# Windowed and latent attention in a macaron network: scores by query in two pairs of head groups, latent jobs first, maxima in three bf16 parts

## The chip, the cores and the metric

One core of a Trainium2 chip runs the whole program. The metric is device time in microseconds, from the start to the end of one execution. The changed kernel is timed against the kernel before on the same chip.

## The reference, cut to what matters

The network is x + 0.5 ffn, x + attention, x + 0.5 ffn, then a ternary layer, a relative-position attention and the ternary layer again. The change lies in the first attention (4 batches of 1024 rows, 256 features). For 16 heads of 16 features it computes, with windows of 64 rows:

```python
Q, K, V = x @ wq, x @ wk, x @ wv                     # 16 heads
sc = Q . K / 4 over this window of 64 keys and the one before, band mask j > i and j <= i + 64
local = softmax(sc) @ V                              # the first window has no window before it
GQ = x @ wgq; GK, GV = pool16(x @ wgk), pool16(x @ wgv)   # 8 latent heads, 64 latents
rem = softmax(GQ . GK / 4, latents of later chunks masked) @ GV @ r_out_w
out = (sigmoid(Q . gl) * local + sigmoid(Q . gr) * rem) @ w_out
```

## The kernel before, in words

The layer is `local_phase` (L387). Four engines run programs written out by hand that meet through semaphores; nothing is reordered. Per batch there are four stages.

**Scores by query.** Eight jobs n = (g, m, e): g is the half of the rows (4 tiles of 128), (m, e) picks four of the 16 heads, one in each row group c of 32 partitions. `scores` (L813) fills the four PSUM banks R[:, 0..3]: a mask matmul for each bank with all 128 rows of the array (L823), then 32 fp32 matmuls of 32 rows and 64 columns (L829), which run as 64 passes. VectorE's `top` (L637) takes the maximum over the keys of all four banks at once (L642). `scores` of the next job waits for it, since it writes the same banks. After each job TensorE runs one of the projections that are left (`project`, L776; the first `EARLY` = 8 of 16 ran in the last stage of the batch before), then `turn_tops` turns the maxima. Two latent jobs follow (`latent_scores` L843, `latent_top` L644).

**Scores by key.** `by_key` (L869), for the same eight jobs: mask (L879), minus the maxima spread over the keys by a selecting matmul in fp32 (`sel`, `mT`, L882), and the scores again with keys on the partitions (L888). ScalarE takes the exponential of the four banks in one instruction (L587). `values` (L905) multiplies with V, VectorE copies (`take`, L652), TensorE turns back (`back`, L930), VectorE divides and gates (`normed`, L664). PSUM Z has four banks for everything that is not scores. The two latent jobs are jobs 8 and 9; their `take` is a reciprocal of 512 elements a row and a product.

**Out.** For 8 tiles `remote`, `turn_out`, `project_out` on TensorE, with the next batch's first 8 projections between them.

The masks are made once, by GpSimd, before batch 0.

Of the kernel before, what the change touches and what calls it, by code (L numbers as in the profile page):

```python
# [7 lines left out]
ALU = mybir.AluOpType  # L8
# [378 lines left out]
def local_phase(nc, G, A):  # L387

    with ExitStack() as ctx:
# [22 lines left out]
        sel = sb("sel", [P, 4, P])  # L412
        sel2 = sb("sel2", [P, 2, NL])
        identb = sb("identb", [P, P], BF)
        maskS = sb("maskS", [P, 2, 512], BF)
        maskT = sb("maskT", [P, 2, 512], BF)
        lmaskS = sb("lmaskS", [P, TPB, P], BF)
        lmaskT = sb("lmaskT", [P, S], BF)
# [13 lines left out]
        mt = sb("mt", [P, TPB, P])  # L432
        mtl = sb("mtl", [P, TPB, P])
        mT = sb("mT", [P, S])
        mTl = sb("mTl", [P, S])
# [13 lines left out]
                 "S smax mtr mTe LS lmax ltr lTe ST sexp PV ot rcp back ri norm E o2 o F Fe out res sums stat")  # L449
# [9 lines left out]
        LAST_V, GATE_JOB, Q_LAST = 11, 12, 6  # L459
# [28 lines left out]
        NMASK = 15  # L488

        @block.gpsimd  # L490
        def _(pool):
            nc.gpsimd.memset(blk[:, :], 1.0).then_inc(s["zero"], 1)
            pool.wait_ge(s["zero"], 1)
            c = Count(s["masks"])

            def keep(t, op, fill, base, pattern, multiplier):
                step(pool, nc.gpsimd.affine_select(out=t, in_=t, compare_op=op, fill=fill, base=base, pattern=pattern,
                                                   channel_multiplier=multiplier), c)
# [8 lines left out]
            nc.gpsimd.memset(mt[:, :, :], 0.0)  # L507
            nc.gpsimd.memset(mtl[:, :, :], 0.0)
            nc.gpsimd.memset(onesB[:, :], 0.0)
            for t in (maskS, maskT, lmaskS):  # L510
                nc.gpsimd.memset(t[:, :, :], 0.0)
            nc.gpsimd.memset(lmaskT[:, :], 0.0).then_inc(s["zero"], 1)
            pool.wait_ge(s["zero"], 3)
            for half in range(2):
                rows = slice(WIN * half, WIN * half + WIN)
                keep(maskS[rows, :, :], ALU.is_gt, NEG, 0, [[0, 8], [1, P]], -1)
                keep(maskS[rows, :, :], ALU.is_ge, NEG, WIN, [[0, 8], [-1, P]], 1)
                keep(lmaskT[rows, :], ALU.is_ge, NEG, 0, [[1, S]], -CHUNK)
            keep(maskT[:, :, :], ALU.is_gt, NEG, 0, [[0, 16], [-1, WIN]], 1)
            keep(maskT[:, :, :], ALU.is_ge, NEG, WIN, [[0, 16], [1, WIN]], -1)  # L520
            keep(lmaskS[:, :, :], ALU.is_ge, NEG, 0, [[P, TPB], [0, 2], [-CHUNK, NL]], 1)
            step(pool, nc.gpsimd.memset(onesB[0:WIN, 0:HD], 1.0), c)
            step(pool, nc.gpsimd.memset(onesB[WIN:P, HD:32], 1.0), c)
            step(pool, nc.gpsimd.memset(maskS[0:WIN, 1, 0:WIN], NEG), c)
            step(pool, nc.gpsimd.memset(maskT[0:WIN, 1, 0:WIN], NEG), c)

        @block.scalar
        def _(act):
# [30 lines left out]
            def top_row(b, g):  # L559
                act.wait_ge(s["mtr"], 2 * b + g + 1)  # L560
                copy(mT[:, 512 * g:512 * g + 512], Z[:, 3, :]).then_inc(s["mTe"], 1)

            def latent_top_row(b, g):
                act.wait_ge(s["ltr"], 2 * b + g + 1)
                copy(mTl[:, 512 * g:512 * g + 512], Z[:, 2, :]).then_inc(s["lTe"], 1)
# [3 lines left out]
            act.wait_ge(s["sels"], 5)  # L569
# [3 lines left out]
            for b in range(B):  # L573
                for j in range(EARLY, NPJ):
                    evacuate(b, j)
                    if j == 13:
                        act.wait_ge(s["pj_d"], dves(b, GATE_JOB))
                        nc.scalar.activation(gt[:, :, :, :], gt[:, :, :, :], ACT.Exp, scale=-1.0).then_inc(s["gexp"], 1)
                for g in range(2):
                    top_row(b, g)  # L580
                for g in range(2):
                    latent_top_row(b, g)
                for n in range(NST):
# [3 lines left out]
                    nc.scalar.activation(PT[:, n % 2, :, :], R[:, :, :], ACT.Exp, scale=0.25).then_inc(s["sexp"], 1)  # L587
                    if b + 1 < B and 4 <= n < 8:
                        xT_out(b + 1, n - 4)
# [7 lines left out]
        def _(dve):  # L597
# [39 lines left out]
            def top(b, n):  # L637
                g, m, e = job(n)
                dve.wait_ge(s["S"], b * NJ + n + 1)
                dst = mt[:, :, :].rearrange("p t (c q) -> p c t q", c=4)[:, :, 4 * g:4 * g + 4, 2 * m + e]  # L640
                src = R[:, :, :].rearrange("p c (t k) -> p c t k", t=4)
                nc.vector.tensor_reduce(dst, src, AX.X, ALU.max, negate=True).then_inc(s["smax"], 1)  # L642

            def latent_top(b, g):  # L644
                dve.wait_ge(s["LS"], 2 * b + g + 1)
                for e in range(2):
                    dst = mtl[:, :, :].rearrange("p t (c q) -> p c t q", c=4)[:, :, 4 * g:4 * g + 4, e]
                    src = R[:, :, :].rearrange("p c (t e n) -> p c t e n", t=4, e=2)[:, :, :, e, :]
                    ins = nc.vector.tensor_reduce(dst, src, AX.X, ALU.max, negate=True)
                ins.then_inc(s["lmax"], 1)  # L650

            def take(b, n):  # L652
                dve.wait_ge(s["PV"], b * NST + n + 1)
                if n < NJ:
                    if n >= 2:
                        dve.wait_ge(s["back"], b * NJ + n - 1)
                    copy(OT[:, n % 2, :], Z[:, 2, :]).then_inc(s["ot"], 1)
                else:
                    nc.vector.reciprocal(rcp[:, n % 2, :], Z[:, 3, :]).then_inc(s["norm"], 1)
                    dve.wait_ge(s["norm"], b * NST + n + 1)  # L660
                    at = (n - NJ) * 512
                    nc.vector.tensor_tensor(remT[:, at:at + 512], Z[:, 2, :], rcp[:, n % 2, :], ALU.mult).then_inc(s["ot"], 1)
# [51 lines left out]
            do(nc.vector.tensor_copy(sel[:, :, :], selr[:, 0:4].unsqueeze(2).to_broadcast([P, 4, P])), "sels", 3)  # L714
            do(nc.vector.tensor_copy(sel2[:, :, :], selr[:, 0:2].unsqueeze(2).to_broadcast([P, 2, NL])), "sels", 4)
            do(nc.vector.tensor_copy(identb[:, :], G.ident[:, :]), "sels", 5)
# [8 lines left out]
            pool_rows(0)  # L725
            dve.wait_ge(s["zero"], 3)
            for b in range(B):
                for n in range(NJ):
                    top(b, n)
                    if n == 5:  # L730
                        evacuate(b, GATE_JOB)
                for g in range(2):
                    latent_top(b, g)
# [3 lines left out]
                for n in range(NST):  # L737
                    if 1 <= n <= NJ:
                        normed(b, n - 1)
                    take(b, n)  # L740
                    if b + 1 < B and n < 4:
                        normalise(b + 1, 2 * n)
                        normalise(b + 1, 2 * n + 1)
                    if b + 1 < B and n == 8:
                        pool_rows(b + 1)
                dve.wait_ge(s["norm"], (b + 1) * NST)
# [14 lines left out]
        def _(pe):  # L761
            mm = nc.tensor.matmul

            def turn(b, g4):
# [4 lines left out]
                elif b >= 1:  # L769
                    pe.wait_ge(s["pj_a"], acts(b - 1, NPJ - 1))  # L770
                    pe.wait_ge(s["pj_d"], dves(b - 1, NPJ - 1))
                for q in range(4):
# [1712 lines left out]
```

## Time and profile before

| | us |
|---|---|
| median of 3 runs | 2364.99 (2362.94 to 2365.01) |
| the profiled execution | 2365.43 |
| its span | 2363.7 |
| scores by query of batch 0, 1, 2, 3 start at | 215.0, 364.2, 507.3, 650.5 |
| the same layer's last output tile is added at about | 791 |

The layer's four batches take 576 us of the span: 149.2, 143.1, 143.1 and 140.8. In rows of a timeline the first number is the start in us from the span's start, the second the duration of the merged instructions from the first start to the last end, then engine, line, operation, tiles, shape and count; brackets give the idle time of the engine before and what ended it. 32*64 means 32 rows and 64 columns of the array. The profile models the ends of matmuls: four of 0.38 us each start 0.22 us apart, so starts are compared, not ends.

### The profile page before, as it was taken

Reading aid. Unit: us, or ns where it says so; the run is one execution under the profiler, and the core shown is the slowest. Engines: PE = TensorE matmul, PEld = TensorE weight load, DVE = VectorE, ACT = ScalarE, POOL = GpSimd, SP = SyncE. Lnnn points to the kernel's source line nnn. Section 1 sums busy time; section 2 is a strip of 40 time slices with the busy share of each in tenths; the row PEclk is TensorE's granted clock in tenths of the full one; section 3 lists DMA queues with packets and bytes.
Section 4 is the critical chain, followed back from the end, with each engine's and each line's share of the span. In section 5 each row is a group of like instructions: output and inputs, shape, how many; then the busy total and the mean of one; then the engine's idle time right before and its main releaser. Section 6 shows DMA issues by size and latency. Waiting matters only on the chain. (4 is left out here: it accounts for less than half of the span.)

```text
span 2363.7 us, 74441 instructions
## 1 busy us (share of the span) xinstructions
PE 2036.5 (86%) x32280; PEld 1279.6 (54%) x32280; DVE 1633.0 (69%) x2585; ACT 1220.4 (52%) x1830; POOL 492.8 (21%) x794
## 2 busy tenths in 40 slices
PE   4986888898888797589986999999999999999985
PEld 2653555555555465445873555555555555555544
DVE  6775355364542677866756888888888888888847
ACT  3761231312212476422423777767776777767754
POOL 0002000000000000000013354435443454445420
PEclk7997899999999899699995999999999999999997
DMA  3001000000000000044358445555554455545412
GB/s 109 1 1 34 13 2 20 2 19 3 1 19 2 1 1 6 1 120 148 142 210 253 112 129 132 133 135 142 136 142 123 118 139 142 136 119 137 109 38 72
DMA packets 273791, 195.11 MB, mean 83 GB/s; under 512 B 206744, under 2 KB 260310, under 8 KB 273210
## 3 DMA queue, kind: packets, MB, share of 16 engines
q1 hardware_dynamic: 262586, 139.27, 23.2%
q0 software_dynamic: 10496, 50.75, 5.7%
q8 instruction: 256, 4.19, 0.8%
q14 instruction: 69, 0.57, 0.1%
q10 hardware_dynamic: 384, 0.33, 0.0%
HBM read 91.69 MB, written 93.88 MB: 79 GB/s over the span
## 5 line engine op out<-in xcount | busy, mean ns | idle before, releaser
L2098 DVE TENSOR_REDUCE a1c_nm<-a1c_S 128x1 f32<-128x1024 f32 x512 | 609.6, 1218 | 83.7 <-PE a1c_S L2185 83.2
L2032 ACT ACTIVATE a1c_PT<-a1c_ST 128x1024 f32<-128x1024 f32 x499 | 509.8, 1022 | 65.9 <-PE a1c_ST L2185 63.0
L2049 ACT ACTIVATE a1c_Pb<-a1c_S,a1c_nm 128x192 f32<-128x192 f32 (+1 forms) x512 | 212.3, 415 | 202.2 <-DVE a1c_nm L2098 201.0
L1971 POOL TENSOR_TENSOR a1c_lt<-a1c_lt 128x256 f32<-128x256 f32 (+5 forms) x448 | 254.0, 567 | 35.5
L2088 DVE COPY a1c_PbT<-a1c_T 96x512 f32<-96x512 f32 x256 | 175.8, 687 | 99.4 <-PE a1c_T L2217 97.0
L2185 PE MATMUL a1c_ST<-a1c_Q,a1c_KR 57*128 57x256 f16 (+2 forms) x1066 | 176.3, 285 | 28.9 <-ACT a1c_PT L2032 19.6
L2185 PE MATMUL a1c_S<-a1c_KR,a1c_Q 54*32 54x512 f16 (+13 forms) x2816 | 181.9, 317 | 14.0 <-DMA a1c_Gx<-a_bias 11.4
L2185 PE MATMUL a1c_S<-a1c_KL,a1c_Q 54*32 54x512 f16 (+11 forms) x3136 | 193.4, 326 | 0.3
L2185 PE MATMUL a1c_S<-a1c_Gx,ident 64*32 64x96 f32 (+2 forms) x4352 | 186.0, 242 | 0.0
L1963 POOL DMA_DIRECT2D a_band<-a1c_Pb x128 | 71.1, 555 | 495.5 <-ACT a1c_Pb L2049 495.4
L2217 PE MATMUL a1c_T<-ident,a1c_Pb 128*96 128x128 f32 x1024 | 169.3, 289 | 0.8 <-DVE a1c_mhl L2112 0.8
L2185 PE MATMUL a1c_ST<-a1c_Q,a1c_KL 57*128 57x128 f16 (+1 forms) x932 | 149.9, 266 | 17.8 <-ACT a1c_PT L2032 16.8
L1055 POOL PARTITION_ALL_REDUCE b_wall<-b_wsum x2 | 0.8, 404 | 785.9 <-DVE b_wsum L1100 785.9
L2217 PEld LDWEIGHTS a1c_T<-ident,a1c_Pb 128*96 128x96 f32 x1024 | 102.7, 129 | 88.8 <-issue 55.7
L587 ACT ACTIVATE a_PT<-a_R 128x2048 f32<-128x2048 f32 x40 | 75.1, 1878 | 146.1 <-PE a_R L888 124.0
L312 DVE TENSOR_TENSOR f_hlo<-f_h,f_hhi 128x512 f16<-128x512 f32 x128 | 88.0, 687 | 70.2 <-ACT f_hhi L230 70.2
L2185 PEld LDWEIGHTS a1c_S<-a1c_Gx,ident 64*32 64x32 f32 x4352 | 126.3, 110 | 13.9 <-issue 0.7
L225 ACT ACTIVATE f_h<-f_psH,b,a 128x512 f32<-128x512 f32 x128 | 99.3, 776 | 60.8 <-PE f_psH L336 59.3
L2185 PE MATMUL a1c_PV<-a1c_PT,a1c_VL 128*17 128x512 f32 (+3 forms) x1280 | 127.4, 470 | 0.2 <-issue 0.2
L2185 PE MATMUL a1c_PV<-a1c_PT,a1c_VU 128*17 128x512 f32 (+3 forms) x1280 | 127.5, 470 | 0.0
L642 DVE TENSOR_REDUCE a_mt<-a_R 128x16 f32<-128x2048 f32 x32 | 73.4, 2293 | 73.9 <-PE a_R L829 73.9
L347 PE MATMUL f_psY<-sw2T,f_hhi 128*128 128x256 f16 x512 | 118.7, 273 | 1.0 <-DVE f_hlo L312 1.0
(353 smaller groups left out, 4088.0 us busy)
## 6 DMA issues: line engine op xcount, KB each, us to landing
a_band<-a1c_Pb POOLq DMA_DIRECT2D x128, 384.0 KB, 3.5
a_bias<-a1b_G SPq DMA_DIRECT2D x32, 768.0 KB, 9.3
a1c_Gx<-a_bias SPq DMA_DIRECT2D x128, 192.0 KB, 4.3
a1c_Dt<-a_band SPq DMA_DIRECT2D x128, 126.0 KB, 3.4
a1c_Q<-a_qk SPq DMA_DIRECT2D x192, 64.0 KB
a1c_Vw<-a_values SPq DMA_DIRECT2D x64, 102.0 KB, 3.0
a1c_KL<-a_qk SPq DMA_DIRECT2D x96, 64.0 KB
a1c_KR<-a_qk SPq DMA_DIRECT2D x90, 64.0 KB
```

What stands on the lines that cost most here:

```text
L225: nc.scalar.activation(h[:, n % NB, :], psH[:, n % NB, :], ACT.Gelu, bias=G.b1[:, m:m + 1], scale=G.a1[:, m:m + 1]).then_inc(s["h"], 1)
L312: nc.vector.tensor_tensor(hlo[:, n % NB, :], h[:, n % NB, :], hhi[:, n % NB, :], ALU.subtract).then_inc(s["hlo"], 1)
L347: last = nc.tensor.matmul(psY[:, i % 2, t, :], x[:, n % NB, t * P:t * P + P], G.sw2T[:, m, :], start=(m + part + t % 2 == 0), stop=(m == M ...
L587: nc.scalar.activation(PT[:, n % 2, :, :], R[:, :, :], ACT.Exp, scale=0.25).then_inc(s["sexp"], 1)
L642: nc.vector.tensor_reduce(dst, src, AX.X, ALU.max, negate=True).then_inc(s["smax"], 1)
L1971: add = lambda o, x, y: nc.gpsimd.tensor_tensor(o, x, y, ALU.add)
L2032: nc.scalar.activation(PT[:, q % 8, :, :], place(q), ACT.Exp).then_inc(s["exp"], 1)
L2049: nc.scalar.activation(Pb[:, band_slot(I, c), w0:w1], SP[:, t % 2, I * P - 32 + w0:I * P - 32 + w1], ACT.Exp, bias=nm[:, t // 16 % 2, col: ...
L2088: nc.vector.tensor_copy(PbT[:, e % RING, :], T[0:BW, :]).then_inc(s["Tb_ev"], 1)
L2098: nc.vector.tensor_reduce(nm[:, t // 16 % 2, col:col + 1], SP[:, t % 2, :], AX.X, ALU.max, negate=True).then_inc(s["max"], 1)
L2185: return nc.tensor.matmul(out, w, x, start=start, stop=stop, skip_group_check=True)
L2217: ins = nc.tensor.transpose(T[0:BW, at:at + P], Pb[:, band_slot(I, c), BW * ch:BW * ch + BW], G.ident[:, :])
```

## The change

- **Order.** The two latent jobs come first: `latent_scores` before the eight jobs by query, latent jobs 0 and 1 of `by_key`, `values` and `take`, local jobs 2 to 9. The job list is put in another order, so that the pooled, latent and first V projections are among the early eight, and two each of Q and K later.
- **Pairs.** In `scores` the four row groups are done as two pairs a = 0, 1. Each pair waits for the maxima of its own pair of the job before, writes its masks and its 16 matmuls, and signals by itself; `top` and `latent_top` reduce in two halves; the exponential is two instructions of half the size, and `by_key` masks each pair of banks behind its own half.
- **Masks.** The band is written by matmuls with 64 rows (`ones64`, `band`) on rows 0 to 63 for even c and 64 to 127 for odd c; in jobs with g = 0 each is followed by a further matmul of 64 rows and 64 columns (`wall`) that masks the missing first window. Latent masks take 32 rows (`of16`, `later`, `laterT`).
- **Maxima.** VectorE splits each maximum in three bf16 parts with four small operations (`in_three`); `mt`, `mT`, `sel`, `sel2` and the turning matmuls are bf16.
- GpSimd makes the new masks in 24 steps in place of 15.

```diff
-        JOBS = [("q", 0, 0), ("k", 0, 0), ("q", 1, 0), ("k", 1, 0), ("q", 0, 1), ("k", 0, 1), ("q", 1, 1), ("k", 1, 1),
-                ("v", 0, 0), ("v", 2, 0), ("v", 4, 0), ("v", 6, 0), ("gate", 0, 0), ("g", 0, 0), ("gq", 0, 0), ("gq", 0, 1)]
+        JOBS = [("q", 0, 0), ("k", 0, 0), ("q", 1, 0), ("k", 1, 0), ("g", 0, 0), ("gq", 0, 0), ("gq", 0, 1), ("v", 0, 0),
+                ("q", 0, 1), ("k", 0, 1), ("q", 1, 1), ("k", 1, 1), ("gate", 0, 0), ("v", 2, 0), ("v", 4, 0), ("v", 6, 0)]
...
             def top(b, n):
                 g, m, e = job(n)
-                dve.wait_ge(s["S"], b * NJ + n + 1)
-                dst = mt[:, :, :].rearrange("p t (c q) -> p c t q", c=4)[:, :, 4 * g:4 * g + 4, 2 * m + e]
+                dst = mx[:, :, :, :].rearrange("p t c q -> p c t q")[:, :, 4 * g:4 * g + 4, 2 * m + e]
                 src = R[:, :, :].rearrange("p c (t k) -> p c t k", t=4)
-                nc.vector.tensor_reduce(dst, src, AX.X, ALU.max, negate=True).then_inc(s["smax"], 1)
+                for a in range(2):
+                    dve.wait_ge(s["S"], 2 * (b * NJ + n) + a + 1)
+                    nc.vector.tensor_reduce(dst[:, 2 * a:2 * a + 2], src[:, 2 * a:2 * a + 2], AX.X, ALU.max, negate=True
+                                            ).then_inc(s["smax"], 1)
...
+            def in_three(whole, left, parts, n, name, value):
+                do(copy(parts[:, :, :, 0:n], whole), name, value + 1)
+                do(nc.vector.tensor_tensor(left, whole, parts[:, :, :, 0:n], ALU.subtract), name, value + 2)
+                do(copy(parts[:, :, :, 4:4 + n], left), name, value + 3)
+                nc.vector.tensor_tensor(parts[:, :, :, 8:8 + n], left, parts[:, :, :, 4:4 + n], ALU.subtract).then_inc(s[name], 1)
...
+            def tri(c):
+                return slice(WIN * (c % 2), WIN * (c % 2) + WIN)
+
             def scores(b, n):
                 g, m, e = job(n)
-                if n == 0:
-                    pe.wait_ge(s["res"], b * TPB)
-                    pe.wait_ge(s["pj_a"], acts(b, EARLY - 1))
-                    pe.wait_ge(s["pj_d"], dves(b, EARLY - 1))
-                else:
-                    pe.wait_ge(s["smax"], b * NJ + n)
+                if n % 2 == 0:
+                    pe.wait_ge(s["pj_a"], acts(b, EARLY + n - 3 if n >= 4 else 3))
+                    pe.wait_ge(s["pj_d"], dves(b, EARLY + n - 3 if n >= 4 else 3))
                 K = KO if e else KE
-                for c in range(4):
-                    mm(R[:, c, :], identb[:, :], maskS[:, int(g == 0), :], start=True, stop=False, skip_group_check=True)
-                for t in range(4):
-                    for half in range(2):
-                        at = (4 * g + t) * P + WIN * half
-                        for c in range(4):
-                            rows = slice(32 * c, 32 * c + 32)
-                            ins = mm(R[WIN * half:WIN * half + WIN, c, t * P:t * P + P], QT[rows, m, at:at + WIN],
-                                     K[rows, m, at:at + P], start=False, stop=True, skip_group_check=True)
-                ins.then_inc(s["S"], 1)
+                for a in range(2):
+                    if n == 0:
+                        pe.wait_ge(s["lmax"], 4 * b + 3 + a)
+                    else:
+                        pe.wait_ge(s["smax"], 2 * (b * NJ + n) - 1 + a)
+                    for c in (2 * a, 2 * a + 1):
+                        mm(R[:, c, :], ones64[tri(c), 0:2, :].rearrange("p a x -> p (a x)"),
+                           band[tri(c), :, :].rearrange("p a x -> p (a x)"), start=True, stop=False, skip_group_check=True)
+                        if g == 0:
+                            mm(R[0:WIN, c, 0:WIN], ones64[tri(c), 0, :], wall[tri(c), :], start=False, stop=False,
+                               skip_group_check=True)
+                    for t in range(4):
+                        for half in range(2):
+                            at = (4 * g + t) * P + WIN * half
+                            for c in (2 * a, 2 * a + 1):
+                                rows = slice(32 * c, 32 * c + 32)
+                                ins = mm(R[WIN * half:WIN * half + WIN, c, t * P:t * P + P], QT[rows, m, at:at + WIN],
+                                         K[rows, m, at:at + P], start=False, stop=True, skip_group_check=True)
+                    ins.then_inc(s["S"], 1)
...
-                    ins = nc.tensor.transpose(Z[:, 3, q * P:q * P + P], mt[:, 4 * g + q, :], G.ident[:, :])
+                    ins = mm(Z[:, 3 - g, q * P:q * P + P], mt[:, 4 * g + q, :, :].rearrange("p c x -> p (c x)"), identb[:, :],
+                             start=True, stop=True, skip_group_check=True)
...
-                    mm(R[:, c, :], identb[:, :], lmaskS[:, 4 * g:4 * g + 4, :].rearrange("p t n -> p (t n)"), start=True,
+                    rows = slice(32 * c, 32 * c + 32)
+                    if g == 1 and c % 2 == 0:
+                        pe.wait_ge(s["lmax"], 4 * b + 1 + c // 2)
+                    mm(R[:, c, :], of16[rows, 0:P], later[rows, 4 * g:4 * g + 4, :, :].rearrange("p t e n -> p (t e n)"), start=True,
                        stop=False, skip_group_check=True)
...
+            def by_key(b, n):
+                for c in range(4):
+                    rows = slice(32 * c, 32 * c + 32)
+                    if c % 2 == 0:
+                        if n == 0:
+                            pe.wait_ge(s["smax"], 2 * (b * NJ + NJ) - 1 + c // 2)
+                        else:
+                            pe.wait_ge(s["sexp"], 2 * (b * NST + n) - 1 + c // 2)
+                    if n < 2:
+                        mm(R[:, c, :], laterT[rows, n, :], of16[rows, :], start=True, stop=False, skip_group_check=True)
+                        continue
+                    mm(R[:, c, :], band[tri(c), 0, :], ones64[tri(c), :, :].rearrange("p a x -> p (a x)"), start=True, stop=False,
+                       skip_group_check=True)
+                    if job(n - 2)[0] == 0:
+                        mm(R[0:WIN, c, 0:WIN], wall[tri(c), :], ones64[tri(c), 0, :], start=False, stop=False, skip_group_check=True)
...
+                for g in range(2):
+                    latent_scores(b, g)
+                    project(b, EARLY + g)
                 for n in range(NJ):
                     scores(b, n)
-                    project(b, EARLY + n)
+                    if n < 6:
+                        project(b, EARLY + 2 + n)
+                    if n == 1:
+                        turn_latent_tops(b)
                     if n == 5:
                         turn_tops(b, 0)
-                latent_scores(b, 0)
-                turn_tops(b, 1)
-                latent_scores(b, 1)
-                turn_latent_tops(b, 0)
-                turn_latent_tops(b, 1)
                 for n in range(NST + 2):
                     if n < NST:
                         by_key(b, n)
-                    if 2 <= n < NJ + 2:
-                        back(b, n - 2)
+                    if n == 0:
+                        turn_tops(b, 1)
+                    if n >= 4:
+                        back(b, n - 4)
...
```

## Rows read from the trace of the kernel before

**Rows 1.** Page, part 2: GpSimd and granted TensorE clock, span in 40 slices of 59 us.

```profile
...
POOL 0002000000000000000013354435443454445420
PEclk7997899999999899699995999999999999999997
...
```

**Rows 2.** Stretches (start:end, length, busy PE, PEld, DVE, ACT, POOL, clock, DMA): batch 1, two of batch 3.

```profile
...
364.20:411.80 47.60, 39.81 (x712) 26.09 (x713) 24.81 (x19) 6.51 (x14) 0.00 (x0) 1.00 0.11 24
411.80:458.60 46.80, 43.03 (x1099) 31.47 (x1096) 14.40 (x52) 17.41 (x12) 0.00 (x0) 1.00 0.01 3
458.60:468.50 9.90, 8.20 (x118) 3.89 (x117) 3.12 (x14) 4.32 (x3) 0.00 (x0) 1.00 0.01 2
468.50:478.10 9.60, 5.36 (x32) 1.13 (x32) 6.75 (x6) 0.03 (x1) 0.00 (x0) 0.82 0.01 2
478.10:507.30 29.20, 27.22 (x100) 16.08 (x96) 18.88 (x43) 7.68 (x16) 0.00 (x0) 1.00 0.00 1
699.70:722.40 22.70, 20.18 (x362) 13.30 (x359) 3.39 (x9) 6.23 (x4) 0.00 (x0) 0.70 0.01 2
770.80:792.00 21.20, 16.02 (x67) 12.55 (x64) 16.74 (x42) 3.07 (x8) 0.00 (x0) 0.82 0.00 1
...
```

**Rows 3.** Timeline, batch 1: last mask, second job by query, next mask; gate projection.

```profile
...
369.44 0.38 PE L823 MATMUL a_R<-a_maskS,a_identb 128*128 128x512 bf16 x1
...
369.75 1.21 PE L829 MATMUL a_R<-a_KO,a_QT 32*64 32x128 f32 x64
...
370.89 1.99 PE L795 MATMUL a_Z<-a_wv,a_xT 128*128 128x256 f32 x8
...
371.00 2.29 DVE L642 TENSOR_REDUCE a_mt<-a_R 128x16 f32<-128x2048 f32 x1 [2.27 <-PE a_R L829]
...
373.35 1.04 PE L823 MATMUL a_R<-a_maskS,a_identb 128*128 128x512 bf16 x4 [0.47 <-DVE a_mt L642]
...
384.58 3.76 PE L809 MATMUL a_Z<-a_gates,a_QT 128*128 128x32 f32 x32
...
```

**Rows 4.** Timeline, batch 1: a job by key, with what follows it.

```profile
...
417.70 1.04 PE L879 MATMUL a_R<-a_maskT,a_identb 128*128 128x512 bf16 x4 [2.00 <-ACT a_PT L587]
...
418.67 1.14 PE L882 MATMUL a_R<-a_mT,a_sel 32*128 32x512 f32 x8
...
419.63 1.91 PE L888 MATMUL a_R<-a_QT,a_KO 32*128 32x64 f32 x64
...
421.61 1.88 ACT L587 ACTIVATE a_PT<-a_R 128x2048 f32<-128x2048 f32 x1 [3.96 <-PE a_R L888]
...
422.70 0.69 DVE L598 COPY a_OT<-a_Z 128x512 f32<-128x512 f32 x1 [9.38 <-PE a_Z L918]
...
427.31 0.66 PE L937 MATMUL a_Z<-ident,a_OT 128*128 128x128 f32 x4
...
```

**Rows 5.** Timeline, batch 1: latent scores and their maxima; the end of the batch.

```profile
...
403.11 1.17 PE L855 MATMUL a_R<-a_GKB,a_GQT 32*128 32x128 f32 x32
...
404.35 2.36 DVE L649 TENSOR_REDUCE a_mtl<-a_R 128x16 f32<-128x1024 f32 x2 [2.56 <-PE a_R L855]
...
468.48 1.07 PE L923 MATMUL a_Z<-a_PT,a_onesB 128*32 128x512 f32 x8 [1.31 <-DVE a_loc L676]
...
470.46 3.36 DVE L659 RECIPROCAL a_rcp<-a_Z 128x512 f32<-128x512 f32 x1 [2.13 <-PE a_Z L926]
...
474.65 1.94 PE L923 MATMUL a_Z<-a_PT,a_onesB 128*32 128x512 f32 x8 [4.24 <-DVE a_remT L662]
...
```

**Rows 6.** Timeline, relative attention: a matmul of 64x128 tiles, then of 64x32.

```profile
...
1702.12 0.27 PE L2185 MATMUL a1c_ST<-a1c_Q,a1c_KL 56*128 56x256 f16 x1
1702.33 0.31 PE L2185 MATMUL a1c_S<-a1c_KR,a1c_Q 54*32 54x320 f16 x2
...
```

**Rows 7.** Page, part 5: an exponential of 1024 elements a row.

```profile
...
L2032 ACT ACTIVATE a1c_PT<-a1c_ST 128x1024 f32<-128x1024 f32 x499 | 509.8, 1022 | 65.9 <-PE a1c_ST L2185 63.0
...
```

**Rows 8.** DMA issues of the layer: count, KB, median us to landing.

```profile
...
a_Vp<-a_V SPq DMA_DIRECT2D x4, 544.0 KB, 6.7
...
```

More of the change, by code:

```diff
@@ L411, in local_phase @@
         selr = sb("selr", [P, 32])
-        sel = sb("sel", [P, 4, P])
-        sel2 = sb("sel2", [P, 2, NL])
+        sel4 = sb("sel4", [P, 4])
+        sel = sb("sel", [P, 4, P], BF)
+        sel2 = sb("sel2", [P, 2, NL], BF)
         identb = sb("identb", [P, P], BF)
[L415 to L418, printed above, removed]
+        ones64 = sb("ones64", [P, 8, WIN], BF)
+        band = sb("band", [P, 4, P], BF)
+        wall = sb("wall", [P, WIN], BF)
+        of16 = sb("of16", [P, 512], BF)
+        later = sb("later", [P, TPB, 2, NL], BF)
+        laterT = sb("laterT", [P, 2, P], BF)
         xn = sb("xn", [P, TPB, D])
@@ L644, in latent_top @@
             def latent_top(b, g):
                 dve.wait_ge(s["LS"], 2 * b + g + 1)
[L646 to L650, printed above, removed]
+                dst = mxl[:, :, 4 * g:4 * g + 4, :].rearrange("p c t e -> p c (t e)")
@@ L652, in take, with split_top, split_latent @@
+            def split_top(b, g):
+                dve.wait_ge(s["smax"], 2 * (b * NJ + 4 * g + 4))
+                rows = slice(4 * g, 4 * g + 4)
+                in_three(mx[:, rows, :, :], rest[:, rows, :, :], mt[:, rows, :, :], 4, "split", 8 * b + 4 * g)
+            def split_latent(b):
+                dve.wait_ge(s["lmax"], 4 * b + 4)
+                in_three(mxl[:, :, :, :].rearrange("p c t e -> p t c e"), rest[:, :, :, 0:2], mtl[:, :, :, :], 2, "lsplit", 4 * b)
             def take(b, n):
@@ new lines, in by_key @@
+            def by_key(b, n):
+                for c in range(4):
+                    rows = slice(32 * c, 32 * c + 32)
+                    if c % 2 == 0:
[10 more added lines that the diff above has]
+                        mm(R[0:WIN, c, 0:WIN], wall[tri(c), :], ones64[tri(c), 0, :], start=False, stop=False, skip_group_check=True)
+                if n < 2:
+                    at = n * 512
+                    pe.wait_ge(s["lTe"], 2 * b + 2)
+                    for c in range(4):
+                        rows = slice(32 * c, 32 * c + 32)
+                        mm(R[:, c, :], sel2[rows, :, :].rearrange("p e n -> p (e n)"), mTl[rows, at:at + 512], start=False,
+                           stop=False, skip_group_check=True)
+                    for c in range(4):
+                        rows = slice(32 * c, 32 * c + 32)
+                        ins = mm(R[:, c, :], GKB[rows, :], GQT[rows, at:at + 512], start=False, stop=True,
+                                 skip_group_check=True)
+                else:
+                    g, m, e = job(n - 2)
@@ L876, in by_key @@
                     pe.wait_ge(s["mTe"], 2 * b + g + 1)
                     K = KO if e else KE
-                    for c in range(4):
-                        mm(R[:, c, :], identb[:, :], maskT[:, int(g == 0), :], start=True, stop=False, skip_group_check=True)
                     for c in range(4):
@@ L981, in _ @@
                         by_key(b, n)
[L982 to L983 removed]
+                    if n == 0:
+                        turn_tops(b, 1)
+                    if n >= 4:
+                        back(b, n - 4)
                     if 1 <= n <= NST:
                         values(b, n - 1)
[L986 to L987 removed]
+                    if b + 1 < B and 5 <= n < 9:
+                        turn(b + 1, n - 5)
                 for t in range(TPB + 2):
```

220 lines of the change are left out of this document (110 added, 110 removed).

## The prediction

> **What bounds it now.** I first read the page's slices of the granted clock [rows 1]: the layer lies between 215 and 791 us, and its slices stand at 0.6 to 0.9 in places and at 9 or more elsewhere. Then I cut batch 1 into its stages [rows 2]. By query, 47.6 us, TensorE busy for 39.8 and VectorE for 24.8; by key, 46.8, TensorE busy 43.0; the two latent jobs 9.9; a tail of 9.6 in which TensorE is busy for 5.4 only; the out stage 29.2, TensorE busy 27.2. So TensorE leads nearly everywhere, but two chains stand in its way, which the timeline shows. By query [rows 3]: masks start at 373.35, having waited for the maximum that began at 371.00 and takes 2.29. By key [rows 4]: the masks at 417.70 waited 2.00 for the exponential of 1.88. In the tail [rows 5] TensorE stands idle for 4.24 behind a reciprocal of 3.36, and the next matmuls take 1.94 instead of 1.07, since the clock has fallen to its lower level, 1.2 GHz (0.82 in the mean of that stretch [rows 2]).
>
> **Prices from rows.** A full mask starts 0.22 after the one before ((1.04 - 0.38) / 3 [rows 3]). A change of the array's tiling costs a pause: the last mask starts at 369.44 and the first 32*64 load at 369.75, 0.31 later where 0.22 is the mask's own [rows 3]: 0.09, and the fp32 weights, now uncovered, 0.05 (64 columns) or 0.10 (128). Columns alone suffice: a 64x128 matmul of 256 columns starts at 1702.12, the 64x32 one at 1702.33 [rows 6], 0.10 after the first's 0.11. The Trainium skill, TensorEngine Tiling (Array Packing), Key Properties, says that changing the tiling mode, not just the tile, drains TensorE, and lists 64x64 and 64x128 as different configurations. It speaks against this change, and would give the sum below and not that of rival B.
>
> A pair of `scores` has 32 passes on 4 tiles; all four groups had 64 on 8. Each tile still makes 8 passes. The latent scores, 32 passes on 4 tiles, take 1.17 - 0.27 = 0.90 from first start to last [rows 5]; the 64 on 8 tiles 1.21 - 0.27 = 0.94 [rows 3]. So a pair costs 0.90 and a job 1.80 where it was 0.94. The other bound is that the time goes with the number of passes, 0.47 a pair, 3.4 us a batch less; the two rows speak for 0.90.
>
> **By query.** A pair with g = 1: change 0.10, two masks side by side 0.22, change and load 0.14, scores 0.90: 1.36, a job 2.7. With g = 0 masks and walls alternate, each a change: 0.10 + 0.22 + 0.11 + 0.03 + 0.10 + 0.22 + 0.11 + 0.03 + 0.14 + 0.90 = 1.96, a job 3.9. A projection is 1.72 (eight passes of 0.22) plus 0.20 for change and load; the gate one 3.8 [rows 3]. Each pair's maximum, 1.2 (half of 2.36 [rows 5]), lies under the other pair and the projection, so VectorE's wait is gone and TensorE alone counts: jobs 4 x 3.9 + 4 x 2.7 = 26.4; projections 7 x 1.9 + 3.8 = 17.1; latent scores 2 x 1.3, of which the second waits 0.7 more for its maxima (2.36 [rows 5], a projection hides 1.9); turning 1.0. Sum 47.8. It was 47.6 with the latent jobs. **Nothing is gained here**: what the wait gave back, the doubled scores and the changes take. The four small operations of each split are hidden by projections, but the last: it delays only `turn_tops(1)`, which job 2 by key needs.
>
> **By key.** Job 0 waits for the last maximum, 1.3. Latent jobs: masks 0.22, `sel2` in bf16 0.22 (one pass; it was two fp32 passes), scores 0.96 as `sel` before, from 418.67 to 419.63 [rows 4]; exponential two halves, at most 2.04 [rows 7]; with the first `values` 7.9 until job 2's masks. A local job now: TensorE's turn (0.6, four passes of 0.11 with change and load) and `values` (1.05: the scores' last passes go in by 421.3, the copy starts at 422.70 with 0.2 for the signal [rows 4]) run during the exponential, then `sel` in bf16 0.22 for 0.96, scores 1.8, changes. g = 1: 0.55 masks + 0.33 + 1.8 + 0.6 + 1.05 + changes = 4.9; TensorE works without a pause, the exponential (2.04 of 4.9) is covered. g = 0: 4 masks one by one 0.88, walls 0.12, nine changes 0.94, then 0.22 + 1.8 + 0.6 + 1.05: 5.7. It was 5.84 (417.70 to 423.54). Four of g = 0: 5.9 (a latent `values` of 1.8, no turn), 5.2, 5.7, 6.3 (with a `turn` of 0.55), 23.1. Three of g = 1 at 4.9 and the last to its end 2.6: 17.3. Then the exponential, `values`, copy, turn, and VectorE's `normed` before the copy: 5.6 to `remote`. Together 7.9 + 23.1 + 17.3 + 5.6 = 53.9, for 46.8 + 9.9 + 9.6 = 66.3 [rows 2]: **12.4 less**. The reciprocals (3.5 + 0.7 twice) now lie on VectorE under jobs 2 to 4; VectorE was busy for 14.4 of 46.8 by key [rows 2], so job 3's `take` comes about in time. What is late without that cover is `values(3)`; I count nothing, at most 2 us a batch.
>
> **Out.** Two of eight projections change from Q and K to the pooled and latent ones: the pooled one has 8 passes of 0.11 instead of 0.22, 0.8 less, and most of TensorE's 2.0 of idle time (29.2 less 27.2 [rows 2]), waits for K copies and for the late reciprocal, goes too. Some 2.1 less, in three batches.
>
> **Before batch 0** GpSimd has 24 steps for 15. Its 0.2 of the slice from 177 us on [rows 1] are 12 to 18 us of masks; a third more ends before the first use at 215: hidden. The copies of V on the SyncE queue go out after the last V projection, which now is the eighth of this stage; they land in 6.7 [rows 8], and two jobs by query and two latent ones, 13 us, lie ahead of their first use. The pooled projection waits 2 us for its sums, a shorter projection and no wait for the last K copy give that back.
>
> **Sum.** 3 x 14.5 + 12.5 = 56; a schedule of all waits with these prices gives 55. Clock: the four tails cost 1.7 each at the lower level, and the idle time ahead of them is gone: 7. Batch 3's jobs by key from 699.7 to 722.4 stood at 0.70 in the mean (three jobs 22.7, where 17.5 is usual), batch 0 had 3 of the same kind, the last out stage ran at 0.82 [rows 2]: I expect as much again and count 1. So 55 + 8 = 63 from the profiled 2365.4: 2302.4. The median stands 0.4 lower: **2302**.
>
> **Rivals.** B: 64 and 64 by 128 tiles are no change of tiling, or the walls go side by side. Then g = 0 pairs cost 1.6, and key jobs 0.7 to 0.9 less: 2302 - 24 = 2278. A pause for columns alone is shown [rows 6], but for 32 columns, not for 64.
> C: waits that I set at nothing bind: the order of VectorE in jobs 2 to 4, the projections' copies between pairs, semaphores ahead of each pair (16 more a batch at 0.1 to 0.3), or the lower clock comes as often in every batch as in batch 3. Half the gain: about 2340.
> D, slower: the lower clock holds through the stages by query. There only half of the array works in a pair, with pauses between. At 1.2 GHz a pass takes twice; batch 3 lost 5.2 in 22.7 us at 0.70, some 0.4 per us at the low level (0.70 is 60% of the time low). A stage of 47.8 us would cost 18 to 38, four of them 70 to 150: 2370 to 2450. It decides from 170 us at the low level on. Against it: the relative attention, whose shapes alternate as in [rows 6], stands at 9 in nearly all slices [rows 1].
> E: the pairs do not overlap with the maxima (the wait for one's own pair is as late as for all): 1.2 a job, 38 in all: 2340, as C.
>
> **Chances.** The forecast 0.60, B 0.15, C and E 0.16, D 0.07, within 0.2% 0.02; 0.2% is about what this measurement can tell. Range: B less a few us of clock at the low end, 2268; C's middle at the high end, 2336; that leaves out C's slower half and D, some 0.17. The likeliest case's own range is 2288 to 2318. Faster 0.91, same 0.02, slower 0.07.
>
> **What would show it.** Stage by query 47 to 49 us a batch, jobs of g = 0 with a projection 5.8 apart, of g = 1 4.6, and no wait of TensorE for maxima but at job 0 by key and the second latent job. Loads of 64*64 and the following 64*128 some 0.1 after the end of the one before: else B. Key jobs 5.7 and 4.9 apart, the tail from the last key scores to `remote` 5.6, batches 128 to 129 us apart. I am wrong if pairs take less than 0.9, if walls cost no change, or if PEclk falls in the stage by query.

## The result, and the profile after

2325.3 us in the median of four runs (2319.9 to 2330.2), the kernel before 2364.0 on the same chip: ratio 0.984, 95% interval 0.981 to 0.986. The forecast was 2302 in a range of 2268 to 2336. The change gains 39 us, not 62. The profiled execution took 2328.2, its span 2326.4.

Stretches of the changed kernel, columns as in [rows 2]: first the stage by query, latent jobs included, of each of the four batches, then the stage by key with its tail of batches 0 and 1, the out stage of batch 1, and the stage by key of batch 3.

```profile
209.20:266.10 56.90, 56.57 (x719) 38.12 (x718) 26.52 (x30) 8.09 (x13) 0.00 (x0) 0.82 0.08 17
347.60:404.30 56.70, 56.44 (x716) 38.35 (x716) 27.45 (x34) 6.20 (x11) 0.00 (x0) 0.82 0.08 17
484.50:538.10 53.60, 53.31 (x718) 35.35 (x718) 27.51 (x34) 6.20 (x11) 0.00 (x0) 0.87 0.08 19
618.30:675.20 56.90, 56.65 (x718) 36.89 (x718) 27.42 (x34) 6.21 (x11) 0.00 (x0) 0.82 0.08 18
266.10:320.40 54.30, 50.44 (x1220) 34.71 (x1221) 27.61 (x70) 22.27 (x25) 0.00 (x0) 0.97 0.02 6
404.30:457.40 53.10, 49.04 (x1225) 34.25 (x1222) 27.66 (x70) 22.27 (x25) 0.00 (x0) 1.00 0.02 6
457.40:484.50 27.10, 25.95 (x106) 16.90 (x104) 16.65 (x49) 7.57 (x19) 0.00 (x0) 1.00 0.00 1
675.20:731.00 55.80, 51.59 (x1204) 33.62 (x1205) 24.51 (x61) 19.87 (x21) 0.00 (x0) 0.91 0.02 5
```

Page of the changed kernel, part 2, as [rows 1]; its 40 slices of 58 us are too coarse to show the fall:

```profile
POOL 0003000000000000000014444435444544445410
PEclk8997898989979996899986999999999999999997
```

The same cut of the kernel before, its four stages by query:

```profile
215.00:265.80 50.80, 42.91 (x712) 27.77 (x713) 24.08 (x16) 7.80 (x15) 0.00 (x0) 0.93 0.10 22
364.20:411.90 47.70, 39.91 (x713) 26.18 (x714) 24.91 (x19) 6.51 (x14) 0.00 (x0) 1.00 0.11 24
507.30:555.00 47.70, 39.90 (x713) 26.18 (x714) 24.91 (x19) 6.51 (x14) 0.00 (x0) 1.00 0.10 24
650.50:699.70 49.20, 41.43 (x712) 26.97 (x713) 24.82 (x19) 6.51 (x14) 0.00 (x0) 0.97 0.10 23
```

The stretches show two things. By key the forecast holds: 53.1 in batch 1, where 53.9 was forecast and 66.3 stood before. By query it doesn't: 56.7 where 47.8 was forecast. TensorE is busy there for 56.44 of 56.70 us, so it hardly waits; but the granted clock is 0.82, where [rows 2] had 1.00. A mean of 0.82 over 56.7 us is 2 x 0.18 x 56.7 = 20 us at the lower level of 1.2 GHz. Cut at the place where it falls and rises:

```profile
347.60:369.80 22.20, 21.94 (x292) 12.47 (x296) 13.82 (x19) 3.51 (x6) 0.00 (x0) 1.00 0.01 2
369.80:390.30 20.50, 20.50 (x166) 15.82 (x162) 5.04 (x9) 1.01 (x2) 0.00 (x0) 0.50 0.00 1
390.30:404.30 14.00, 14.00 (x274) 10.06 (x266) 8.58 (x7) 1.68 (x3) 0.00 (x0) 1.00 0.30 66
```

Timeline of the changed kernel, batch 0: a job with g = 0 at the upper clock, then the gate projection at the lower.

```profile
216.16 0.39 PE L870 MATMUL a_R<-a_band,a_ones 64*128 64x512 bf16 x1
216.48 0.21 PE L873 MATMUL a_R<-a_wall,a_ones 64*64 64x64 bf16 x1
216.62 0.39 PE L870 MATMUL a_R<-a_band,a_ones 64*128 64x512 bf16 x1
216.94 0.21 PE L873 MATMUL a_R<-a_wall,a_ones 64*64 64x64 bf16 x1
217.09 1.10 PE L880 MATMUL a_R<-a_KE,a_QT 32*64 32x128 f32 x32
218.12 0.39 PE L870 MATMUL a_R<-a_band,a_ones 64*128 64x512 bf16 x1
...
234.30 7.04 PE L851 MATMUL a_Z<-a_gates,a_QT 128*128 128x32 f32 x32
```

And a job by key of the same batch, beside [rows 4]:

```profile
281.24 0.39 PE L931 MATMUL a_R<-a_ones,a_band 64*128 64x512 bf16 x1
281.38 3.36 DVE L689 RECIPROCAL a_rcp<-a_Z 128x512 f32<-128x512 f32 x1 [1.61 <-PE a_Z L987]
...
283.09 0.39 PE L952 MATMUL a_R<-a_mT,a_sel 32*128 32x512 bf16 x4
...
283.32 1.90 PE L958 MATMUL a_R<-a_QT,a_KO 32*128 32x64 f32 x64
...
285.29 1.94 ACT L596 ACTIVATE a_PT<-a_R 128x1024 f32<-128x1024 f32 x2 [3.82 <-PE a_R L958]
...
286.38 0.39 PE L931 MATMUL a_R<-a_ones,a_band 64*128 64x512 bf16 x1
```

`sel` takes 283.32 - 283.09 = 0.23 where it was 0.96, the next job starts 5.14 after this one, and the reciprocal of 3.36, which TensorE waited for in [rows 5], lies under the masks and scores. By query, the pair takes 218.12 - 216.16 = 1.96, the forecast's number; the gate projection 7.04 where [rows 3] had 3.76.

**Where the time went.** Profile against profile: before the layer 5.8 less (first stage by query at 209.2, was 215.0); the four stages by query 224.1 for 195.4, 28.7 more; by key with the tails 216.2 for 272.8, 56.6 less; the out stages 95.5 for 107.0, 11.5 less; after the layer 1581.5 for 1573.5, 8.0 more. Sum 37.2 less; the spans differ by 37.3. The 8.0 after the layer is not owed to the change: the same kernel took about 1576 there in its second profile (e11). Before the layer some 5 of the 5.8 is clock, 42 us at the lower level (granted 0.90 of 209.2 us) for 52 (0.88 of 215.0).

### The profile page after: what moved, and what is told of

It is laid out like the page before. It is cut to its first block and busy times, and to the rows that moved or that the text cites. A ratio compares the mean times of both kernels' runs of the same rounds, so it can differ in the third digit from the quotient of the medians.

```text
span 2326.4 us, 74481 instructions
## 1 busy us (share of the span) xinstructions
PE 2058.9 (89%) x32248; PEld 1314.9 (57%) x32248; DVE 1646.0 (71%) x2668; ACT 1222.7 (53%) x1870; POOL 497.0 (21%) x804
## 5 line engine op out<-in xcount | busy, mean ns | idle before, releaser
L596 ACT ACTIVATE a_PT<-a_R 128x1024 f32<-128x1024 f32 x80 | 77.5, 1021 | 131.8 <-PE a_R L958 94.3
L655 DVE TENSOR_REDUCE a_mx<-a_R 128x8 f32<-128x1024 f32 x64 | 78.5, 1226 | 83.8 <-PE a_R L880 81.7
```

The lines of the kernel that those rows point to most:

```text
L596: nc.scalar.activation(PT[:, n % 2, 2 * a:2 * a + 2, :], R[:, 2 * a:2 * a + 2, :], ACT.Exp, scale=0.25).then_inc(s["sexp"], 1)
L655: nc.vector.tensor_reduce(dst[:, 2 * a:2 * a + 2], src[:, 2 * a:2 * a + 2], AX.X, ALU.max, negate=True).then_inc(s["smax"], 1)
```

## The experiments

The texts put down before the runs name these theories. L: the clock falls because a pair uses half of the array. M: it falls because of the many changes of tiling. G: because of the gate projection. W and P: the clock has no part, only the prices of pairs count. T: it holds where TensorE streams for long without small matmuls and changes.

All kernels but e4 are made from the changed one. The table gives for each the median and the ratio to the kernel before on its chip; the length of the four stages by query in the profiled execution; how much of that was at 1.2 GHz ("low"), which is 2 x (1 - granted clock) x length, summed over the four; the same for the rest of the layer, from the end of each stage by query to the beginning of the next or to the end of the layer; and what a stage by query would last at 2.4 GHz: a quarter of the length less half of the low time. For the kernel before, the last four are 195.4, 10, 41 and 47.6.

| | median | ratio (95%) | by query | low | low, rest of layer | at 2.4 GHz |
|---|---|---|---|---|---|---|
| changed (first) | 2325.3 | 0.984 (0.981, 0.986) | 224.1 | 75 | 14 | 46.6 |
| e11 changed, again | 2325.8 | 0.985 (0.984, 0.987) | 227.4 | 81 | 21 | 46.7 |
| e1 unsplit | 2290.0 | 0.970 (0.968, 0.973) | 185.9 | 30 | 32 | 42.7 |
| e2 wide walls | 2273.6 | 0.964 (0.961, 0.967) | 187.5 | 34 | 31 | 42.6 |
| e7 walls after masks | 2291.2 | 0.972 (0.969, 0.974) | 194.1 | 42 | 10 | 43.3 |
| e5 e1 and e2 | 2251.9 | 0.955 (0.952, 0.958) | 162.6 | 12 | 40 | 39.2 |
| e8 e5, two jobs paired | 2242.2 | 0.952 (0.949, 0.955) | 155.9 | 6 | 27 | 38.2 |
| e9 e8, spread | 2244.6 | 0.951 (0.949, 0.954) | 167.2 | 31 | 0 | 38.0 |
| e3 gate last | 2340.9 | 0.990 (0.986, 0.994) | 233.0 | 93 | 42 | 46.7 |
| e4 before, with pairs | 2403.2 | 1.018 (1.011, 1.024) | 203.0 | 75 | 31 | 41.4 |
| e6 full filler | 2340.8 | 0.993 (0.991, 0.996) | 242.1 | 48 | 0 | 54.5 |
| e12 half filler | 2357.0 | 0.999 (0.998, 1.001) | 271.8 | 118 | 10 | 53.2 |
| e10 idle rows filled | 2338.7 | 0.990 (0.988, 0.992) | 237.2 | 73 | 42 | 50.2 |

In e4 the stage is without the latent jobs, which stand apart there. Three profiled executions lay some 9 us above their medians: e2, e10, e12; their low time is by so much the less typical. The two profiles of the changed kernel differ by 6 us of low time by query and by 7 in the rest, so smaller differences say nothing. The runs stand on several chips, on which the kernel before took 2357.8 to 2364.0; a difference of two medians can be off by as much. And the last column counts half of the low time as lost, which is too much where TensorE waits in it: the stage by query of batch 1 stood at 1.00 in e5 and in e8 (below, after that of e1) and took 39.8 and 38.2; batch 3 of e9 stood at 1.00 and took 39.1, where the column has 38.0.

```profile
342.70:388.80 46.10, 42.20 (x716) 27.11 (x716) 26.74 (x35) 6.20 (x11) 0.00 (x0) 0.93 0.11 25
331.80:371.60 39.80, 35.39 (x716) 23.20 (x716) 26.72 (x35) 6.20 (x11) 0.00 (x0) 1.00 0.13 29
326.30:364.50 38.20, 37.15 (x718) 24.74 (x718) 26.79 (x34) 6.20 (x11) 0.00 (x0) 1.00 0.12 26
```

**e1, unsplit.**

```diff
-                for a in range(2):
-                    ... masks and scores of c in (2 * a, 2 * a + 1)
+                for c in range(4):                 # masks, each half behind its own maxima
+                    ...
+                for t in range(4):
+                    for half in range(2):
+                        for c in range(4):
+                            ins = mm(...)
+                ins.then_inc(s["S"], 2)
```

> The changed kernel with the scores by query of a job formed again as one block of four head groups (64 passes on 8 tiles behind all four masks), masks still behind the maxima of their own half. Theory L, the low clock of the stage by query comes from pairs, which use half of the array: the granted clock stays at its upper level there, the stage falls from 56 to some 48 us (jobs of g = 0: 2.8 of masks, walls and changes, 1.9 of projection, 0.3 of wait; of g = 1: 1.9 + 1.9 + 0.8) and the whole to about 2295. Rival M, it comes from the many changes of tiling (9 in a job of g = 0 here, 10 in the changed kernel): the clock falls as in the changed kernel, 20 us low a batch, and the time stays within 10 of 2325. Rival W, the clock has nothing to do with it and only the prices of pairs count: also 2325 or a little above, since two maxima are waited for again in jobs 6 and 7.

Measured 2290.0: 35 less (31 by the ratios). The whole advantage lies by query, 224 -> 186, by the table 4 x 3.9 = 16 of it at the upper clock and (75 - 30) / 2 = 22 from the clock. The low time didn't vanish, and in the rest of the layer there was more of it (32 for 14 and 21), so theory L as stated is not the whole; rival M, that nothing would change, is out, and so is W, which had no part for the clock.

**e2, walls in the band's shape.** The same is done in `by_key`.

```diff
-                            mm(R[0:WIN, c, 0:WIN], ones64[tri(c), 0, :], wall[tri(c), :], ...)
+                            mm(R[:, c, 0:WIN], onesL[tri(c), :], wall[tri(c), 0:WIN], ...)   # columns 64 to 127 of onesL are 0
```

> The changed kernel with each wall as a matmul with a 64x128 tile, the shape of the band's, so that mask and wall are one tiling (the added half is zeros). At the upper clock a pair of g = 0 takes 1.96 - 0.3 and a key job of g = 0 some 0.8 less: 5.8 a batch, 23 in all. Theory L (half-used array): the low clock stays where it is, some 20 us a batch, and the time is about 2300. Rival M (changes of tiling bring the low clock): it goes too, and the time is 2275 or less.

Measured 2273.6: 52 less, as rival M had it (2275 or less) and below L's 2300; but the low clock, which by M goes, only shrank. Timeline of this kernel, the same job:

```profile
219.41 0.39 PE L876 MATMUL a_R<-a_band,a_ones 64*128 64x512 bf16 x2
219.64 0.20 PE L879 MATMUL a_R<-a_wall,a_onesL 64*128 64x64 bf16 x2
219.77 1.10 PE L886 MATMUL a_R<-a_KE,a_QT 32*64 32x128 f32 x32
220.80 0.39 PE L876 MATMUL a_R<-a_band,a_ones 64*128 64x512 bf16 x2
```

A pair takes 1.39, not 1.96: of one tiling, the two masks run side by side in 0.23 and both walls take 0.13. I had forecast 0.3 less; it is 0.57, twice the columns in 0.71 of the time. The low time by query halved as well (75 -> 34), with the pairs still there: so the changes of tiling have a part in it. Part of it moved, though: the first 10 us of the stage by key, at 1.00 in batch 1 of the changed kernel, stood lower in batches 1 to 3, and the whole layer has 65 us of low time for 89. Batch 1 of e2:

```profile
383.90:394.00 10.10, 8.24 (x48) 2.75 (x48) 4.02 (x7) 3.83 (x5) 0.00 (x0) 0.58 0.06 15
```

**e3, gate projection last.** `JOBS` ends in `..., ("v", 2, 0), ("v", 4, 0), ("v", 6, 0), ("gate", 0, 0)]`.

> The changed kernel with the gate projection (64 passes of 32 columns) moved from the place after job 2 by query to that after job 5, behind the three V projections. Rival G, the gate projection brings the low clock: the low stretch begins some 14 us later in each batch and is shorter by as much, the time falls by 5 to 15. Theory L: it begins at the same place, in or before job 3, and the time is within 5 of 2325.

Neither: 2340.9, 15 more, in runs from 2317 to 2352. The clock fell at 371.9, 16 us into the stage of batch 1 and long before the gate projection (which started at 400.44), and again at 402.6, just after it had begun. So the gate projection isn't what starts it, against rival G, but with it moved there was more of it (93 for 75 and 81).

**e4, the kernel before with pairs alone.**

> The kernel before with one thing of the change: scores by query as two pairs of head groups, each behind the maxima of its own pair (full 128x128 masks as before, no other reordering). At the upper clock a job costs 0.44 + 0.24 + 0.90 twice and 1.9 of projection, 5.1 where it was 5.9: the stage 47.6 -> 42 us, the whole 2345. Theory L: the low clock comes in these stages here too, some 15 to 20 us a batch, which costs 6 to 8 a batch: 2365 to 2380. Rivals M and G: no low clock (few changes; the gate projection is there in the kernel before too), 2345.

2403.2, 44 slower than before, above even L's figure. My 5.9 for a job before was wrong: it took 4.56, from its first mask at 368.79 to that of the next job at 373.35 ([rows 3] show its last mask, at 369.44). In the profile of e4 a job in pairs takes 382.19 to 387.15, 4.96 where 5.1 was forecast. The first line is of the kernel before, the others of e4:

```profile
368.79 1.04 PE L823 MATMUL a_R<-a_maskS,a_identb 128*128 128x512 bf16 x4 [0.47 <-DVE a_mt L642]
```

```profile
382.19 0.38 PE L826 MATMUL a_R<-a_maskS,a_identb 128*128 128x512 bf16 x1
...
383.54 0.60 PE L826 MATMUL a_R<-a_maskS,a_identb 128*128 128x512 bf16 x2
...
385.11 1.99 PE L797 MATMUL a_Z<-a_wv,a_xT 128*128 128x256 f32 x8
...
387.15 0.38 PE L826 MATMUL a_R<-a_maskS,a_identb 128*128 128x512 bf16 x1
```

So pairs lose by themselves: the wait that they remove was 0.47 a job, the scores, on half of the tiles at a time, cost 0.86 more (1.80 for 0.94), and a job is 0.40 longer. At the upper clock the stage is 41.4 for 37.9, 14 us in four, and 75 us of low clock, where these stages had 3, cost 36 more: 50 by these prices, 44 measured. The low clock comes with pairs where no wall and no new order is; but each pair brings changes of tiling of its own, between its mask and its scores.

**e7, walls after both masks of a pair**, by query only: three changes of tiling a pair, not five.

> The changed kernel with only this altered: by query the two walls of a pair stand behind both masks, so a pair of g = 0 has three changes of tiling where it had five, and its two masks go side by side. Price of changes: 0.1 twice and 0.15 of overlap, 0.35 a pair, 2.8 a batch at the upper clock, 11 in all: 2312 to 2316, and about 1 a batch more if the low clock shrinks with it. If changes of tiling are not what costs: 2325.

2291.2, 34 less, 21 below the expected range. At the upper clock 3.3 a batch less (2.8 expected), 13; the low time 75 -> 42 gives 17. **e5, e1 and e2 together:**

> Both of the first two edits together: scores by query as one block of four head groups, and walls in the band's tile shape. If the two gains are of different things (half-used array; changes of tiling), they add, less what VectorE's maxima (2.4 a job, behind a projection of 1.9) hold back by query: by key 0.8 less in four jobs a batch, 13 in all, by query up to 10: 2268 to 2280, with no more low clock than in the unsplit kernel. If both only bring the clock back, the second adds nothing: 2285 or more.

2251.9, 16 below the lower end. Most of the two gains adds: (2325 - 2290) + (2325 - 2274) = 86 by simple addition, 73 measured. By query 12 us of low clock are left, but 40 came in the rest of the layer; with 51 together the layer is back at what it had in the kernel before. **e8**, pairs only where no projection follows (`if n < 6`: unsplit):

> As the unsplit and wide kernel, but jobs 6 and 7 by query, which have no projection behind them to cover the maxima, stay two pairs each. Unsplit, such a job waits for its maxima: 0.94 + 2.4 + 0.4; in pairs it takes 2.7, so 0.9 a job and some 7 in all is to be gained at the upper clock. If a pair pays where nothing else covers the maxima: 5 to 8 below the unsplit and wide kernel. If the low clock comes with even two such jobs, then no gain or a loss of up to 10.

2242.2, 10 below e5, where 5 to 8 was forecast, and with e9 the fastest of all, 5% below the kernel before. At 1.00 a stage by query went from 39.8 to 38.2, 6 us in four. **e9**, jobs 3 and 7 in pairs:

```diff
-                    if n < 6:
-                        project(b, EARLY + 2 + n)
+                    if n in PROJ_AT:     # PROJ_AT, PAIRS_AT = (0, 1, 2, 4, 5, 6), (3, 7)
+                        project(b, EARLY + 2 + PROJ_AT.index(n))
```

> The mixed kernel (unsplit where a projection follows, pairs where none does, walls in the band's shape) with the projections by query spread: after jobs 0, 1, 2, 4, 5 and 6, and jobs 3 and 7 in pairs, where they were after jobs 0 to 5 and jobs 6 and 7 in pairs. At the upper clock the same sum. If it is stretches of pairs, small matmuls and waits in a row that bring the low clock, the one of 10 us at the beginning of the stage by key (batches 1 and 3 of the mixed kernel) goes or shrinks: 5 to 12 faster than the mixed kernel. If the place of the projections doesn't matter: within 3 of it. Against both: the last V projection now ends one job later, and the copies of V may be waited for, up to 2 a batch.

2244.6, the same as e8. The low clock at the beginning of the stage by key did go (27 us in the rest of e8's layer, 0 in e9's), but nearly as much came by query (6 -> 31): moved, not removed.

**What the clock follows.** e6 adds full matmuls to each pair, e12 equally long ones on half of the rows, e10 passes on the idle rows in the first pair of each job; e11 is the changed kernel beside e10.

```diff
+                    for c in (2 * a, 2 * a + 1):                                            # e6
+                        mm(R[:, c, :], identb[:, :], of16[:, :], start=True, stop=False, ...)
+                    for _ in range(2):                                                      # e12
+                        mm(R[:, 2 * a, :], ones64[tri(0), 0:2, :]..., band[tri(0), :, :]..., start=True, stop=False, ...)
+                            for c in (2, 3) if a == 0 else ():                              # e10, beside each pass
+                                mm(Z[WIN * half:WIN * half + WIN, 2 + c % 2, t * P:t * P + P], QT[rows, ...], K[rows, ...], ...)
```

> The changed kernel with work added that nobody needs: in each pair two full 128x128 matmuls of 512 columns in bf16 ahead of the masks, which overwrite what they wrote. At the upper clock that is 0.44 and one more change, 0.5 a pair, 8 a batch, 35 in all: 2360 if the low clock stays as it is or has nothing to do with how full the array is. Theory L (the clock falls since the array is half used): the low clock of the stage by query goes or shrinks, which gives back up to 10 a batch: 2320 to 2335, more matmuls in the time of fewer.

> The changed kernel with 32 passes that nobody needs beside the 32 of the first pair of each job: the same scores on the two row groups that stand idle there, into two other banks. They run beside the pair's own and cost nothing but two waits for those banks (job 2 for a latent row's copy, job 6 for a row's copy), at most 1 a batch; masks, walls and changes of tiling stay. Theory L, the clock falls because half of the array is idle: with half of the pairs filled, the low clock by query, 75 us in four batches, goes down towards the 29 of the unsplit kernel, and the time to 2300 to 2315. Rival M (changes of tiling, small walls) and rival P (only the time of pairs): low clock and time stay, 2322 to 2330.

> The changed kernel itself once more, beside the others on one chip, for its time and its low clock there: 2320 to 2330, 14 to 21 us of low clock in each stage by query.

> The filler again, with half of the array: in each pair two matmuls of 512 columns that nobody needs, as 64x128 tiles of one half of the rows, one behind the other, where the filler kernel had two of 128x128. The same time at the upper clock (0.44 a pair, 7 a batch, 28 in all) without a change of tiling more. If what the clock follows is how much of the array works (theory L), the low clock by query stays at the 75 to 82 us of the changed kernel: 2350 to 2358. If it is how long TensorE streams without small matmuls and changes (theory T), it falls as with the full filler, to some 50 us: 2335 to 2345.

The fillers part the theories. At the upper clock e6 costs 7.8 a batch and e12 6.5, as they should; yet e6, 2340.8, is only 15 us above the changed kernel (20 by the ratios), since the low time sank (75 to 81 -> 48, and 14 to 21 -> 0 in the rest of the layer). It lies between L's range, which it misses by 6, and the 2360 of no effect. e12, 2357.0, is 31 above, in L's range and above T's, with no less low time (118 in an execution 9 above the median). e11 came in at 2325.8 as expected, with 17 to 27 us of low clock a stage where 14 to 21 was. The stage by query of batch 2 in e6, then those of batches 1 and 2 in e12, the first of which had the least low time of its four:

```profile
495.10:554.80 59.70, 58.91 (x742) 36.01 (x750) 27.48 (x34) 6.20 (x11) 0.00 (x0) 0.91 0.08 19
```

```profile
362.80:424.80 62.00, 61.71 (x748) 38.10 (x748) 27.51 (x34) 6.20 (x11) 0.00 (x0) 0.86 0.08 18
505.10:574.90 69.80, 69.54 (x750) 41.31 (x750) 27.43 (x34) 6.20 (x11) 0.00 (x0) 0.76 0.07 16
```

That speaks for the used part of the array (L) and against the mere length of a stream (T). e10 speaks against L in its simple form: with the idle rows at work in half of the pairs, the low time stayed (73 for 81), the stage cost 3.5 a batch more at the upper clock where 1 was expected (the pair with 64 passes 1.14 for 1.03, and the two waits), and the time rose by 13, to 2338.7, above the ranges of all theories. So added full bf16 matmuls brought the clock back in part, added fp32 passes on the idle rows didn't.

What is shown: by query the low clock shrinks when pairs are undone and the walls stay (e1), when walls change shape or place and pairs stay (e2, e7), and comes when pairs alone are added (e4). Pairs were not tested apart from the changes of tiling that they bring. The number of these doesn't order the runs by itself: counted from the order of the matmuls, a batch's jobs by query have some 50 in e1 and 32 in e4, with 30 and 75 us of low time. Nor is it enough that TensorE hardly waits: in batch 1 of e8 it was busy for 37.15 of 38.20 us at 1.00. Which property of pairs and changes the clock answers to stays open.

## Why the forecast was right in sign and 23 us too low

- **The step that failed** is "by query: nothing is gained here", 47.8 us a batch: the sum was made at 2.4 GHz. At that clock the four stages come to 46.6 each, 1.2 below the sum; 75 us at the lower level make them 56.0. The mis-sized term is rival D's, which I gave 0.07 and treated as all or nothing, with 170 us as its threshold. It came with 75 us, cost 37, and took more than half of what the stage by key gained. Against the sum of 63 us: by query 28.7 more where nothing was put; by key 56.6 less, as put; out 11.5 less for 6.3; before and after the layer together 2.2 more, where nothing was put. That leaves 37. My argument against it, that the relative attention's alternating shapes keep the clock, compared other work.
- **The price of a low us.** I wrote 0.4 per us; in a stage where TensorE is busy throughout it is 0.5: the passes take twice as long (gate projection 7.04 for 3.76).
- **Pairs.** 0.90 for 32 passes on 4 tiles holds (pair of g = 0 1.96; 1.96 forecast), and so does "the wait for maxima is gone". But undone, they give 3.9 a batch at the upper clock (e1), and alone they cost 14 us and the clock (e4). Where a projection covers the maxima, halving the tiles buys nothing; in jobs 6 and 7, where none does, pairs gain (e8, 1.6 a batch at 1.00).
- **Changes of tiling.** Rival B is out: each wall costs its pause. First the row: mask to wall 0.31 or 0.32, wall to mask 0.14 to 0.15. The Trainium skill, TensorEngine Tiling (Array Packing), Key Properties, says that changing the tiling mode drains TensorE. The trace agrees: the wall starts 0.10 later than the mask's own 0.22. What I had not priced is that the changes also keep the two row groups from working side by side: 0.57 a pair in e2, 4.0 a batch by query, and 41 us of low clock by query, of which 17 came back in the rest of the layer.
- **By key.** 53.9 forecast, 53.1 and 53.0 in batches 1 and 2. Local jobs with g = 0 started 5.76, 5.14, 5.51 and 6.10 apart (5.9, 5.2, 5.7, 6.3 forecast), the first two of g = 1 4.8 (4.9). The reciprocals lie under other work as described.
- **Out and edges.** 2.0 a batch less in three, as forecast; the last one 5.5 less, since its clock is 1.00 and was 0.82 [rows 2]; I had counted on the same clock again, so this is luck. Before the layer 5.8 less, which I had put at nothing; after it 8.0 more at a granted clock of 0.94 for 0.95, in code that is the same. That these two nearly cancel is luck too.
- **Clock of the tails.** By key the four stages fell by 56.6; less 12.4 x 4 = 49.6 from work, that leaves the 7 us forecast. It is a remainder, not measured by itself; the low time of the rest of the layer fell from 41 us to 14.
- **Rival C and E.** No wait for maxima by query but at the second latent job. C's figure of 2340 is nearer than the forecast, for a reason that its first half doesn't name; its last clause, lower clock more often, is the one that holds.

## What to carry to other kernels

When a split doubles the time of matmuls on the engine that bounds the stage, ask what else covers the wait that it removes; if something does, only split where nothing does. Keep neighbouring small matmuls in one tile shape, even at twice the columns with zeros. And make the sum at both clocks: a stage in which TensorE hardly waits can still fall to 1.2 GHz, as this one, filled with small tiles, did. When a variant shows less low time in one stage, look for it in the next (e2, e5, e9).

## What the runs showed of the hardware

- The granted clock fell while TensorE was busy for 21.94 of the 22.20 us before and for all of the 20.50 us in which it stayed low. The Trainium skill, TensorE: Matmul & The Clock Gate, HAM oscillation, ties such a fall to gaps in which the engine idles; here the longest idle time in these 42.7 us was 0.26.
- Work that nobody needs can be half paid by the clock: two full matmuls a pair, 7.8 a batch at 2.4 GHz, cost 15 to 20 us in four batches, not 31 (e6).
- A wall of twice the columns in the mask's shape made a pair 0.57 us shorter (e2).
